# Perceiver layer on Trainium2: three biases added to the residual by GpSimd instead of by matmuls of ones

## What is computed

```python
x = x + _L0_xattn_ref(_layernorm(x), ctx_768, w_q, w_kv, w_out, b_out)   # ... out @ w_out + b_out
x = x + _L0_attn_ref(_layernorm(x), ..., Wk, Wv, Wr, Wo, bo)             # ... (r * wkv) @ Wo.T + bo
x = x + _L0_ffn_ref(_layernorm(x), w1, b1, w2, b2)                       # ... relu(h @ w1 + b1) @ w2 + b2
```

## Time and profile before

| | |
|---|---|
| median of 3 runs | 2463.47 us (2462.11 to 2464.36) |
| the profiled execution | 2464.89 us, its span 2463.1 us |
| the part that the change touches | 2104 to 2463 us |
| PE busy over the whole span | 95% |
| DVE / ACT / POOL busy over the span | 67% / 60% / 64% |
| granted TensorE clock, mean | 0.983 |

### The profile page before, as it was taken

How to read it: one execution, slowest core, us unless ns; L and a number is a source line. 1 busy time by engine, 2 the same in 40 slices (tenths; PEclk the granted TensorE clock), 3 DMA queues, 4 the chain that set the end, 5 groups by cost and what they waited for, 6 DMA issues and landing times. The chain is left out here.

```text
span 2463.1 us, 42955 instructions
## 1 busy us (share of the span) xinstructions
PE 2347.1 (95%) x14000; PEld 2143.9 (87%) x14000; DVE 1649.8 (67%) x2650; ACT 1486.0 (60%) x2433; POOL 1566.4 (64%) x786
## 2 busy tenths in 40 slices
PE   4969999999999999999999999999999997499999
PEld 3648999999999999999999999999999997388788
DVE  7766666666666666666666666666666664568873
ACT  4655666666666666666666666666666663355343
POOL 2006888888888888888888888888888874100000
PEclk9989999999999999999999999999999998699999
DMA  5857878888888888878888888888888864775000
GB/s 155 255 171 179 196 193 194 194 193 197 196 197 196 198 193 197 192 194 194 194 193 195 195 194 194 194 194 198 198 196 194 193 163 96 183 198 151 1 10 26
DMA packets 376472, 433.83 MB, mean 176 GB/s; under 512 B 80054, under 2 KB 347356, under 8 KB 376412
## 3 DMA queue, kind: packets, MB, share of 16 engines
q1 hardware_dynamic: 376412, 433.06, 71.8%
HBM read 162.34 MB, written 52.43 MB: 87 GB/s over the span
## 5 line engine op out<-in xcount | busy, mean ns | idle before, releaser
L555 POOL TENSOR_TENSOR p_pt_lo<-p_landed,p_pt_hi 128x768 fp32r<-128x768 f32 (+1 forms) x512 | 1005.2, 1985 | 357.8 <-ACT p_pt_hi L619 357.8
L794 PE MATMUL p_acc<-p_nat,p_pt_hi 128*128 128x384 f32 x3328 | 975.9, 361 | 13.6 <-POOL p_pt_lo L555 13.3
L796 PE MATMUL p_acc<-p_nat,p_pt_lo 128*128 128x192 f32 x3328 | 844.6, 254 | 0.0
L651 ACT ACTIVATE p_prob<-p_scores,p_negmax 128x800 f32<-128x800 f32 (+1 forms) x512 | 471.2, 926 | 516.3 <-DVE p_negmax L724 516.3
L778 PE MATMUL p_scores<-p_ct_hi,p_q_hi 128*128 128x512 f32 (+2 forms) x2048 | 710.1, 350 | 24.2 <-DVE p_ct_hi L751 13.8
L778 PE MATMUL p_scores<-p_ct_hi,p_q_lo 128*128 128x512 f32 (+2 forms) x2048 | 705.1, 348 | 0.0
L730 DVE STREAM_TRANSPOSE turned<-p_prob 128x1664 f32<-128x1664 f32 x256 | 489.5, 1912 | 317.0 <-ACT p_prob L651 317.0
L794 PEld LDWEIGHTS p_acc<-p_nat,p_pt_hi 128*128 128x128 f32 x3328 | 629.1, 189 | 16.0 <-issue 13.7
L796 PEld LDWEIGHTS p_acc<-p_nat,p_pt_lo 128*128 128x128 f32 x3328 | 639.3, 192 | 0.0
L619 ACT ACTIVATE p_pt_hi<-p_landed 128x768 fp32r<-128x768 f32 (+1 forms) x512 | 432.3, 892 | 158.0 <-PE p_acc L796 150.6
L778 PEld LDWEIGHTS p_scores<-p_ct_hi,p_q_hi 128*128 128x128 f32 x2048 | 388.8, 190 | 72.1 <-issue 14.3
(11 more groups left out here) (193 smaller groups left out, 2394.8 us busy)
## 6 DMA issues: line engine op xcount, KB each, us to landing
p_landed<-turned SPq DMA_DIRECT2D x2048, 104.0 KB, 2.2
shared<-in_ctx SPq DMA_DIRECT2D x96, 312.0 KB
o_scratch<-shared SPq DMA_DIRECT2D x256, 96.0 KB, 2.6
qk_scratch<-p_out_a SPq DMA_DIRECT2D x16, 1024.0 KB, 4.6
p_raw<-o_scratch SPq DMA_DIRECT2D x32, 512.0 KB, 4.4
p_stage<-qk_scratch SPq DMA_DIRECT2D x31, 512.0 KB, 3.8
p_stage<-qk_scratch SPq DMA_DIRECT2D x62, 256.0 KB, 4.2
p_stage<-in_ctxT SPq DMA_DIRECT2D x31, 401.0 KB, 3.3
```

What stands on the lines that cost most here:

```text
L555: nc.gpsimd.tensor_tensor(pt_lo[:, t0:t1, :, :], by_tile(slot, t0, t1), bits(pt_hi[:, t0:t1, :, :]), ALU.subtract).then_inc(pt_lo_done, 1)
L651: nc.scalar.activation(prob[:, lo:hi], scores[:, S0 + lo:S0 + hi], ACT.Exp, bias=negmax[:, par:par + 1], accum_out=rowsum[:, par, h:h + 1] ...
L794: nc.tensor.matmul(acc[k % 2][:, 0:2 * DC], pt_hi[:, t, :, :].rearrange("p i x -> p (i x)"), x[:, t, :], start=t == 0, stop=False, skip_gr ...
L796: last = nc.tensor.matmul(acc[k % 2][:, 0:DC], pt_lo[:, t, :, :].rearrange("p i x -> p (i x)"), x[:, t, 0:DC], start=False, stop=t == KT - ...
```

## The change

The tile `ones`, the split of the biases and the 48 matmuls of ones go; the first matmul of each bank now carries the start flag itself. Each bias is loaded once, broadcast to 128 partitions (three DMAs of 128 KB into a `bias` tile of 128 x 3 x 256). After its old work POOL adds a bias to a chunk of the residual, in place and 128 x 1024 at a time, 12 times: `to_x(c)` adds `b_out` once `x` has landed, `to_mixed(c)` adds `bo` after `normal(0, c)`, `to_fed(c)` adds `b2` after `normal(1, c)`. DVE's `add_attended`, `add_mixed` and `add_fed` wait for the add that belongs to them.

```diff
-        bias, ones = sb("bias", [BR, 3, DM], F32R), sb("ones", [BR, P], F32R)
+        bias = sb("bias", [P, 3, DM])
...
-            sp.wait_ge(bias_zero, 1)
             for n, v in enumerate((b_out, bo, b2)):
-                for row in (0, BR - 1):
-                    sp.dma_start(bias_raw[row:row + 1, n, :], v.rearrange("(a n) -> a n", a=1)).then_inc(b_in, 16)
+                sp.dma_start(bias[:, n, :], v.partition_broadcast(P)).then_inc(b_in, 16)
...
-            nc.gpsimd.memset(bias_raw, 0.0).then_inc(bias_zero, 1)
-            nc.gpsimd.memset(bits(ones[:, :]), 1.0).then_inc(pads_zero, 1)
...
+            def add_bias(c, which, done):
+                tiles = resid[:, c * CTT:(c + 1) * CTT, :]
+                row = bias[:, which:which + 1, :].broadcast_to([P, CTT, DM])
+                nc.gpsimd.tensor_tensor(tiles, tiles, row, ALU.add).then_inc(done, 1)
+
+            def to_x(c):
+                pool.wait_ge(x_in[c], 16)
+                if c == 0:
+                    pool.wait_ge(b_in, 3 * 16)
+                add_bias(c, 0, x_biased)
+
+            def to_mixed(c):
+                pool.wait_ge(xn_done, (turn_of(0, c) + 1) * CTT)
+                add_bias(c, 1, mixed_biased)
+
+            def to_fed(c):
+                pool.wait_ge(xn_done, (turn_of(1, c) + 1) * CTT)
+                add_bias(c, 2, fed_biased)
+
+            to_x(0); to_x(1); to_mixed(0); to_mixed(1); to_x(2); to_x(3); to_mixed(2); to_fed(0); to_mixed(3); to_fed(1); to_fed(2); to_fed(3)
...
-            def biases():
-                low = slice(BR - 1, BR)
-                dve.wait_ge(b_in, 6 * 16)
-                nc.vector.tensor_copy(bias[:, :, :], bias_raw).then_inc(bias_done, 1)
-                dve.wait_ge(bias_done, 1)
-                nc.vector.tensor_tensor(bias[low], bias_raw[low], bits(bias[low]), ALU.subtract).then_inc(bias_done, 1)
...
             def add_attended(c):
-                dve.wait_ge(x_in[c], 16)
+                dve.wait_ge(x_biased, c + 1)
...
             def add_mixed(c, half):
+                dve.wait_ge(mixed_biased, c + 1)
...
             def add_fed(c):
+                dve.wait_ge(fed_biased, c + 1)
...
-            def biased(t, which):
-
-                nc.tensor.matmul(sums[t // 2][:, t % 2 * DM:(t % 2 + 1) * DM], ones[:, :], bias[:, which, :], start=t % 2 == 0, stop=False,
-                                 skip_group_check=True)
...
-                    if j == 0:
-                        biased(t, 0)
+
                     tok = slice(t * P, (t + 1) * P)
                     for m, (a, w) in enumerate(((at_hi, wo_hi), (at_hi, wo_lo), (at_lo, wo_hi))):
-                        last = nc.tensor.matmul(sums[t // 2][:, t % 2 * DM:(t % 2 + 1) * DM], a[:, s, tok], w[:, j, :], start=False,
+                        last = nc.tensor.matmul(sums[t // 2][:, t % 2 * DM:(t % 2 + 1) * DM], a[:, s, tok], w[:, j, :],
+                                                start=j == 0 and m == 0 and t % 2 == 0,
                                                 stop=j == HP - 1 and m == 2, skip_group_check=True)
```

More of the change, by code:

```diff
@@ L835, in finish_layer @@
     RAW, HIDS = 3, 3
-    BR = 33
     PADQ = NQ + 1
@@ L887, in finish_layer @@
         w1_raw, w2_raw = high_half.rearrange("p (k n) -> p k n", n=WIDTH), high_half.rearrange("p (f n) -> p f n", n=DM)
-        bias_raw = er[0:BR, :, :].rearrange("p o n -> p (o n)")[:, 0:3 * DM].rearrange("p (m n) -> p m n", n=DM)
         sums = [pb(f"sums{i}", [P, 512]) for i in range(2)]
@@ L901, in finish_layer @@
         w1_hi_done, w1_lo_done, w2_hi_done, w2_lo_done = sem("w1_hi"), sem("w1_lo"), sem("w2_hi"), sem("w2_lo")
-        ident_done, bias_zero, pads_zero, bias_done = sem("ident"), sem("bias_zero"), sem("pads_zero"), sem("bias")
+        ident_done, pads_zero = sem("ident"), sem("pads_zero")
+        x_biased, mixed_biased, fed_biased = sem("x_biased"), sem("mixed_biased"), sem("fed_biased")
         td_done, decay_done = sem("td"), sem("decay")
@@ L1072, in e_key @@
                 if c == 0 and o == 0:
-                    act.wait_ge(pads_zero, 3 + 2 * KB)
+                    act.wait_ge(pads_zero, 2 + 2 * KB)
                 if c > 0:
@@ L1080, in e_rec @@
                 act.wait_ge(mix_ready[RECEPTANCE], g + 1)
-                if c == 0 and o == 0:
-                    act.wait_ge(bias_done, 2)
                 if c > 0:
@@ L1280, in hidden_lo @@
                 nc.vector.tensor_tensor(hid_lo[n % HIDS], hid[n % HIDS], bits(hid_hi[n % HIDS]), ALU.subtract).then_inc(hid_lo_done, 1)
-            value_weights(); value_weights_lo(); lo(0); lo(1); out_weights_lo(); biases(); mix_shares(); lo(2); at(0); at(1)
+            value_weights(); value_weights_lo(); lo(0); lo(1); out_weights_lo(); mix_shares(); lo(2); at(0); at(1)
             lo(3); lo(4); at(2); lo(5); mix_weights_lo(); at(3); lo(6); at(4); lo(7); at(5); lo(8); at(6); at(7); lo(9); at(8)
@@ L1333, in y @@
                     pe.wait_ge(wo_lo_done, 1)
-                    pe.wait_ge(pads_zero, 1)
-                    pe.wait_ge(bias_done, 2)
                 if j == 0 and c > 0:
@@ L1368, in mix @@
                     pe.wait_ge(sq_lo_done, 13)
-                    pe.wait_ge(pads_zero, 3)
+                    pe.wait_ge(pads_zero, 2)
                 if o == 0 and m == KEY:
@@ L1391, in mixed_out @@
                     tok, dst = slice(t * P, (t + 1) * P), tp[:, t % 2 * DM:(t % 2 + 1) * DM]
-                    nc.tensor.matmul(dst, ones[:, :], bias[:, 1, :], start=t % 2 == 0, stop=False, skip_group_check=True)
                     for k in range(KB):
                         for m, (a, w) in enumerate(((wkv_hi, mo_hi), (wkv_hi, mo_lo), (wkv_lo, mo_hi))):
-                            last = nc.tensor.matmul(dst, a[:, k, tok], w[:, k, :], start=False, stop=k == KB - 1 and m == 2, skip_group_check=True)
+                            last = nc.tensor.matmul(dst, a[:, k, tok], w[:, k, :], start=k == 0 and m == 0 and t % 2 == 0,
+                                                    stop=k == KB - 1 and m == 2, skip_group_check=True)
                 last.then_inc(g_done, 1)
@@ L1422, in feed_out @@
                 for t in range(CTT):
-                    if f == 0:
-                        biased(t, 2)
                     tok = slice(t * P, (t + 1) * P)
                     for m, (a, w) in enumerate(((hid_hi, w2_hi), (hid_hi, w2_lo), (hid_lo, w2_hi))):
-                        last = nc.tensor.matmul(sums[t // 2][:, t % 2 * DM:(t % 2 + 1) * DM], a[s][:, tok], w[:, f, :], start=False,
+                        last = nc.tensor.matmul(sums[t // 2][:, t % 2 * DM:(t % 2 + 1) * DM], a[s][:, tok], w[:, f, :],
+                                                start=f == 0 and m == 0 and t % 2 == 0,
                                                 stop=f == FB - 1 and m == 2, skip_group_check=True)
```

## The result

| | before | after |
|---|---|---|
| median | 2464.49 us (6 runs, 2462.11 to 2466.45) | 2444.66 us (6 runs, 2443.13 to 2449.66) |
| ratio | | 0.9924, 95% interval 0.9911 to 0.9936 |
| the profiled execution, its span | 2464.89, 2463.1 | 2443.13, 2441.0 |

The change makes the kernel faster by 19.8 us, 0.8%. The forecast was 2452.7: direction and range hold, and the size does not, as 10.8 us were forecast. The time lies at the foot of the range, outside the forecast's own case (2446 to 2458.5) and next to rival (a), 2441.

What follows compares the result with a forecast made beforehand. PE was taken to bound most stretches after 2104 us, DVE 2234 to 2300. Terms -1.9 + 1.7 - 2.0 + 1.9 - 10.5 = -10.8 us, from the median 2463.5 to 2452.7; range 2443 to 2461.

Steps and rivals of the forecast that it cites:

- the forecast's own case: Whole kernel: 2452.7 us, reaching from 2446 to 2458.5 as single terms may be off by a microsecond or two; chance 0.60.
- rival (a): DVE absorbs the adds, losing only 1.5 us at 2234 to 2300 and 1 at 2345: gain 22, 2441 us; chance 0.15.
- A matmul of ones costs 0.50 us: On PE, each of 48 ones-matmuls costs 0.50 us through the change between 128 and 33 weight rows: 24.0 us removed.
- The first stretch: 2104 to 2151 us: `y(0)` gains 2.0, `biases()` 0.8, and `to_x(0)` costs 0.9; net -1.9 us.
- The second stretch: 2151 to 2183 us: `to_x(1)` leaves 0.7 of `y(8)`'s 2.0, `to_mixed(0)` makes PE wait 2.4; net +1.7 us.
- The third stretch: 2183 to 2234 us, PE sets the pace: `y(16)` gains 2.0, `to_mixed(1)` falls into idle time; net -2.0 us.
- The fourth: 2234 to 2300 us, DVE bounds: PE's 4.0 us gain all lost, `to_x(2)`, `to_x(3)` and `to_mixed(2)` delay DVE; net +1.9 us.
- 0.4 late: 2234 to 2300 us: after `to_x(2)` and `to_x(3)` cost 4.5, DVE is 0.4 us late instead of gaining 2.2.
- The last: 2300 to 2463 us: 28 matmuls gain 14.0, adds cost 3.5, 3 of it at 2330 to 2354; net -10.5 us.
- The lock: Each POOL add holds the SBUF ports shared with DVE, delaying DVE's two-input or scale-and-shift SBUF work by up to 2.4 us.
- (b): Adds replace the matmuls: 12 exposed whole give +4.0, 2467.5 us, or 2475.8 at 3.1 each; chances 0.15 and 0.06.
- (c): The ones-matmul gap belongs to the start of a sum and moves to the next matmul: about 2465 us; chance 0.04.

Runs made afterwards that it cites:

- eight held back: The changed kernel with eight of its twelve POOL adds each waiting further, until a DVE reciprocal or gap: 2441.00 us, ratio 0.9900.

## Why the prediction was right in direction and range, and half in size

**A matmul of ones costs 0.50 us.** Right, and the strongest term: the removal came to 24.9 us by the medians, 24.8 forecast gross. That the row count is the reason was shown by the runs with 64, 65 and 128 rows, and that the time goes on both sides of the matmul by the timeline; that it is the change, and not 64 rows or fewer as such, is likely and was not tested apart. The Trainium skill ("TensorEngine Tiling (Array Packing)", section "Tiling Modes") says that a change of tiling mode drains TensorE and lists modes of 128, 64 and 32 rows; that 64 rows behave as 33 and 65 as 128 agrees with it, with 0.86 against 0.48 us.

**The first stretch.** -3.3 in place of -1.9. Of `biases()` I had counted 0.8 us, as the input of `lo(2)` was there only at 2126.29. In the changed kernel and in the one without adds that input came earlier against the start of the stage, and `v(2)` began 2.6 and 2.4 us sooner, which is more than the whole of `biases()`. Part of this is chance: the load in front of it took 6.2 us without adds and 7.9 with eight held back. Over all profiled executions `v(2)` began 25.8 to 26.8 us after the first fill in the five kernels with `biases()` and 23.6 to 26.1 in the seven without, 1.7 sooner in the mean. So `biases()` was probably worth about its full 1.8 us, and not 0.8. `to_x(0)` cost 2.1 and not 0.9: `x` landed just as `lo(5)` was done, in front of the run of twelve low parts.

**The second stretch,** the first step that failed. I had POOL slip between the halves of `lo(12)` and PE wait 2.4 us at `v(12)`. It did not: POOL waited 1.5 us, DVE lost 0.2. The loss through `to_x(1)` was right in its place and size (1.8 us of DVE). From `v(6)` to `v(12)` `y(8)` gave exactly its 2.0 us and the adds took 1.6 back, where the forecast had 1.3 for `to_x(1)` and 2.4 for `to_mixed(0)`. The second stretch is off by 2.0 us for this reason.

**The third stretch.** Right: `to_mixed(1)` falls mostly into the gap, and -2.0 was measured as forecast.

**The fourth.** -1.2 in place of +1.9. DVE does bound it, and of 4.0 us taken from PE even the kernel without adds keeps only 3.1. The adds took 2.8 back, and 0.8 came from a higher clock at `v(25)`. `to_x(2)` ran beside the reciprocal and took 0.5 from DVE, `to_x(3)` 1.6: 2.1 for the two in place of 4.5. The forecast had `x` land at 2259, when the reciprocal was just over; it landed while it ran. `to_mixed(2)` with 1.8 was right. The forecast's "0.4 late" does not follow from its row either: 4.5 less the gap of 3.47 is 1.0.

**The last.** -13.6 in place of -10.5. The 28 matmuls gave their 14.0 (14.1 measured), and the adds cost 1.6 in place of 3.5: 1.0 at `to_mixed(3)` and 0.6 at `to_fed(2)`. The other 1.2 us are the clock: the 60 matmuls behind the turn took 11.8 us at a mean clock of 0.87 in the kernel before and 10.6 at 1.00 in the changed one. They took 10.6 as well in the kernel with all matmuls of ones and adds of zeros, so this is hardly a gain of the change. I counted 3 of 4 us lost to DVE between 2330 and 2354. `to_fed(1)` did fall into DVE's full run, but DVE's run was not interrupted: POOL waited 2.8 us. So the term mis-sized in the second and the last stretch is one and the same: that DVE pays for a collision. It was half right. At `to_mixed(0)` and `to_fed(1)`, where DVE went first, it paid 0.2 and 0.0 (at `to_fed(2)`, where POOL let four instructions pass and then began, still 0.8), and POOL, which nobody waited for, paid 7.9 us over all twelve (36.6 - 12 x 2.39).

**The lock.** L262 and L755, which gave the price, were both cases in which POOL had won. Both showed truly how long DVE waits then, 1.6 to 2.1 us here, but not how often. The changed kernel's 10.2 us are 0.85 for each add, and about 5 came out in the time, 0.4 for each: the forecast had 14.0 us between its gross 24.8 and its net 10.8, nearly three times as much. The Trainium skill ("SBUF — State Buffer", "SBUF: two separate sides") says that whoever starts first has the ports for the whole instruction and the other blocks fully. The trace agrees where DVE waits: L1179 at 2165.21 took 3.04 us in place of 1.22, until the add was over. Where POOL waits it agrees only in part, as POOL let five of DVE's instructions pass and not one (5.19 us in place of 2.39). What decides at the border of two instructions the runs do not settle: in the kernel with doubled adds POOL got in between the halves of `lo(10)` and not between those of `lo(12)`. It is no chance, though: `to_fed(1)` took 5.18 or 5.19 us in every kernel with whole adds in which it was not held back.

**The rivals.** (a) came nearest, with 2441 for 2444.7, and each of its reasons holds in part: only 10.2 of 28.8 us fell on DVE, and about half of these came out in the time. (b), that the adds take the place of the matmuls, is false for twelve adds and true for twenty-four: the kernel with doubled adds is within 0.05% of the one before. Its point of decision was 2.07 us exposed for each add; measured were 0.4 for the first twelve and 1.7 for the next. (c) is refuted.

## What to carry to other kernels

Cost a small matmul by the distance between starts with and without it, not by its own row, and look at its row count: here 32 rows of zeros more (65 in place of 33) gave 18 us with no new work on any engine. Work moved to GpSimd in place on SBUF is not free because GpSimd is idle: list what VectorE does at each release, and hold it back until a reciprocal or a gap. Such collisions are cheap while TensorE has cover and dear afterwards, so the first dozen tells little about the next. And before a difference of a microsecond between two traces is explained, compare the granted clock in the pieces right behind TensorE's waits.

## What the runs showed of the hardware that was not expected

- A matmul with 64 rows of weights between matmuls of 128 rows costs 0.50 us, one with 65 rows 0.12; both have 256 columns at the full clock.
- GpSimd, once it has to wait, may wait for a whole run of VectorE's instructions with two inputs in SBUF: for five in a row (2.8 us) at 2339.89, at the same place in every kernel where that add was not held back.
- The same 60 matmuls behind the turn took 10.6 us at a mean granted clock of 1.00, and 11.6 at 0.88, after waits of nearly the same length (2.69 us without adds, 2.68 with eight held back). What made the difference is open.
